# Two gates carried in the rows of a gather table, degrees summed by pairs, and a part of a product moved from VectorE to ScalarE, in a graph network with mixture-of-experts layers

## The reference

```
x = x + gnn0(LN(x))   # product with W, mean over the edges into dst, batch norm, relu
x = x + ffn0(LN(x))   # 256 -> 1024 gelu, top 1 of 8 experts 1024 -> 256
x = x + gnn1(LN(x))   # deg = segment_sum(weight, src) + 1; sum over edges of a src of
                      # LN(x)[dst] * weight * deg^-1/2 * deg^-1/2, then three 256x256 products
x = x + ffn1(LN(x))   # top 2 of 8 experts, softmax of the two logits as gates,
                      # 256 -> 512 relu -> 256
```

## Time and profile before

| | |
|---|---|
| runs | 3897.34, 3900.81, 3908.94 us; median 3900.81 |
| the profiled execution | 3894.43 us, its span 3892.7 us |
| granted TensorE clock, mean | 0.863 |
| busy: PE, DVE, POOL, ACT | 77%, 64%, 59%, 26% of the span |
| first sum | about 116 to 1465 us |
| second sum | about 2235 to 3289 us |
| rest of the last heads and routing | 3289 to 3375 us |
| slots of ffn1 | 3375 us to the end |

### The profile page before, as it was taken

The page is one execution under the profiler, slowest core; times in us unless marked ns, Lnnn a source line. Parts: engine busy times, 40 slices in busy tenths (PEclk is TensorE's granted clock), DMA queues, the critical chain, the costliest instruction groups (busy, mean ns, idle before and its releaser), DMA issues.

```text
span 3892.7 us, 48961 instructions
## 1 busy us (share of the span) xinstructions
PE 2981.4 (77%) x13242; PEld 2223.9 (57%) x13242; DVE 2487.6 (64%) x6393; ACT 1021.9 (26%) x2553; POOL 2284.8 (59%) x2223
## 2 busy tenths in 40 slices
PE   6776766677777777999799077777777776699897
PEld 5665655567676645666688044444544454566554
DVE  5688888898888868664522566666666665633332
ACT  5553433444444415433011200000000000022221
POOL 1676655677777770000244077777777774577776
PEclk9786677899989988999799578888788887799999
DMA  5332222233333332222244433444344445433332
GB/s 160 99 103 85 79 63 64 75 86 86 88 88 87 89 89 76 103 109 98 85 150 135 156 111 116 116 121 116 116 116 121 117 116 85 138 55 55 54 54 44
DMA packets 188761, 380.01 MB, mean 98 GB/s; under 512 B 42140, under 2 KB 113192, under 8 KB 188105
## 3 DMA queue, kind: packets, MB, share of 16 engines
q0 software_dynamic: 121488, 285.06, 28.4%
q1 hardware_dynamic: 58072, 82.67, 6.0%
q10 hardware_dynamic: 8928, 9.04, 0.8%
HBM read 301.05 MB, written 77.44 MB: 97 GB/s over the span
## 4 chain that ended last, share of the span: by engine, by line
PE 44%; DVE 22%; issue 14%; POOL 9%; DMA 8%; DVEq 1%; ACT 1%; SPq 0%; POOLq 0%
PE bank L766 17%; DVE acc_or_weights L733 6%; DMA ring_or_weights<-gather_table,item_other_node 5%; PE bank L1566 5%; PE bank L1383 4%; PE bank L1195 4%; PE bank L934 3%; POOL out_rows L1982 3%; POOL ring_or_weights L777 3%; PE bank L1398 2%; PE bank L1756 2%; POOL normed L1959 2%; PE bank L998 2%; DVE normed L918 2%; DVE acc_or_weights L878 1%
## 5 line engine op out<-in xcount | busy, mean ns | idle before, releaser
L777 POOL DMA_INDIRECT ring_or_weights<-gather_table,item_other_node x1660 | 1664.4, 1003 | 723.6 <-issue 387.2
L733 DVE TENSOR_TENSOR acc_or_weights<-bank,acc_or_weights 128x257 f32 (+1 forms) x1660 | 703.2, 424 | 568.6 <-PE bank L766 479.8
L766 PE MATMUL bank<-ring_or_weights,normed 128*128 128x257 f32 x1660 | 666.0, 490 | 235.2 <-issue 146.2
L766 PE MATMUL bank<-ring_or_weights 128*128 128x256 f32 x1660 | 627.0, 488 | 268.7 <-DVE acc_or_weights L733 96.9
L766 PEld LDWEIGHTS bank<-ring_or_weights 128*128 128x128 f32 x1660 | 319.0, 227 | 537.4 <-issue 286.8
L987 ACT ACTIVATE acc_or_weights<-iota_row,ring_or_weights 128x128 f32<-128x128 f32 x782 | 315.1, 403 | 633.0 <-PE bank L998 623.8
L766 PEld LDWEIGHTS bank<-ring_or_weights,normed 128*128 128x128 f32 x1660 | 307.5, 230 | 287.8 <-issue 273.9
L998 PEld LDWEIGHTS bank<-normed,acc_or_weights 128*128 128x128 f32 x1564 | 352.3, 229 | 78.5 <-ACT acc_or_weights L989 4.6
L934 PE MATMUL bank<-normed 128*128 128x128 f32 x1564 | 254.5, 313 | 139.1 <-DVE normed L922 138.5
L1195 PE MATMUL bank<-identity,normed 128*128 128x128 f32 x1764 | 266.8, 284 | 105.7 <-DVE normed L573 48.6
L1195 PEld LDWEIGHTS bank<-identity,normed 128*128 128x128 f32 x1764 | 213.3, 147 | 187.7 <-issue 82.7
(11 more groups left out here) (337 smaller groups left out, 3955.5 us busy)
## 6 DMA issues: line engine op xcount, KB each, us to landing
ring_or_weights<-gather_table,item_other_node POOLq DMA_INDIRECT x1660, 2.8
hidden_rows<-normed SPq DMA_DIRECT2D x49, 512.0 KB, 2.6
acc_or_weights<-in_L_ffn_Wd SPq DMA_DIRECT2D x8, 1024.0 KB, 5.4
acc_or_weights<-in_L_ffn_W SPq DMA_DIRECT2D x16, 512.0 KB, 9.8
gather_table<-normed SPq DMA_DIRECT2D x7, 896.0 KB, 4.2
gather_table<-acc_or_weights SPq DMA_DIRECT2D x7, 896.0 KB, 4.0
gather_table<-normed SPq DMA_DIRECT2D x24, 256.0 KB, 2.3
out_rows<-x_rows SPq DMA_DIRECT2D x24, 256.0 KB
```

Of the source, the lines that this page charges most:

```text
L733: v.tensor_tensor(into, bank[i % nbank][:, 0:width], into, ALU.add).then_inc(added, 1)
L766: m.matmul(bank[i % nbank][:, 0:width], lhsT=hot, rhs=ring[:, i % RING, 0:width], start=True, stop=True).then_inc(sum_made, 1)
L777: g.indirect_dma_start(ring[:, i % RING, 0:D], None, table, IndirectOffsetOnAxis(ap=gidx[:, i:i + 1], axis=0)).then_inc(ring_in[i % RING], 16)
```

## The change

- **Degrees by pairs.** Two columns of edges are taken together: the one-hots of the tile of both (98 columns) are the weights, and the one-hots of the row of both (256 columns) stream. PE makes 391 products of 98 x 256 instead of 782 of 128 x 49. ScalarE still makes |iota - row| for each column, but relu once for a pair. The sum holds the wanted degrees in two blocks, which two matmuls add at the start of the batch norm stage.
- **A product on ScalarE.** In `spread_edges` the product of lane one-hot and edge values is made by ScalarE (8 activations of 64 columns with a scale read from memory) for all four columns of the first 28 batches and for two of four afterwards. PE sums a batch three items after DVE's step instead of one, and the merge comes two items later.
- **Heads.** Steps fall by 16.5 items for each tile instead of 17, with 12 more items allowed instead of 10. Two steps are added: 11 (Exp on ScalarE) and 12 (three small operations on DVE), which make the head's gates. Items behind the last real one now add to a tile of their own behind tile 48.
- **Gates in the rows.** `tab2` has rows of 258 values: 256 normed and the two gates. A head is stored to it once its gates are there, and after its x. The gate table, its transposes, its store and the 105 gathers of gates are gone. In the slot loop DVE takes the right one of the two gates from the gathered row with two operations on one column.

```diff
-PER_TILE = -(-ITEMS // T)
-MARGIN = 10
+HALVES = 33
+MARGIN = 12
...
-    tab2 = scratch_dram("gather_table2", (T * P, D))
+    tab2 = scratch_dram("gather_table2", (T * P, D + 2))
...
-        v.tensor_scalar(cf, ti, float(T - 1), float(AW), ALU.min, ALU.mult).then_inc(cf_ready, 1)
+        v.tensor_scalar(cf, ti, float((T - 1, T)[k]), float(AW), ALU.min, ALU.mult).then_inc(cf_ready, 1)
...  spread_edges
-        vs.then(v.tensor_tensor(lane_hot[:, 0:n, :], iota[:, 0:LO].unsqueeze(1).broadcast_to([P, n, LO]),
-                                lane_of[:, cols].unsqueeze(2).broadcast_to([P, n, LO]), ALU.is_equal))
-        v.tensor_tensor(spread[:, b % 2, 0:n, :, :], lane_hot[:, 0:n, :].unsqueeze(3).broadcast_to([P, n, LO, 2]),
-                        rec1[:, cols, :].unsqueeze(2).broadcast_to([P, n, LO, 2]), ALU.mult).then_inc(spread_made, 1)
+        if b >= 2:
+            v.wait_ge(spread_scaled, b - 1)
+        lane = lane_hot[b % 2]
+        v.tensor_tensor(lane[:, 0:n, :], iota[:, 0:LO].unsqueeze(1).broadcast_to([P, n, LO]),
+                        lane_of[:, cols].unsqueeze(2).broadcast_to([P, n, LO]), ALU.is_equal).then_inc(spread_made, 1)
+        a = by_scalar(b)
+        if a < n:
+            v.wait_ge(spread_made, lanes_count(b))
+            rest = slice(cols.start + a, cols.stop)
+            v.tensor_tensor(spread[:, b % 2, a:n, :, :], lane[:, a:n, :].unsqueeze(3).broadcast_to([P, n - a, LO, 2]),
+                            rec1[:, rest, :].unsqueeze(2).broadcast_to([P, n - a, LO, 2]), ALU.mult).then_inc(spread_made, 1)
+
+    def by_scalar(b):
+        return min(GC if b < SLOW else GC // 2, batch_columns(b).stop - b * GC)
+
+    def scale_edges(b):
+        s.wait_ge(spread_made, lanes_count(b))
+        if b >= 2:
+            s.wait_ge(spread_summed, b - 1)
+        for c in range(by_scalar(b)):
+            for r in range(2):
+                last = s.activation(spread[:, b % 2, c, :, r], lane_hot[b % 2][:, c, :], ACT.Copy,
+                                    scale=rec1[:, b * GC + c, r:r + 1])
+        last.then_inc(spread_scaled, 1)
...  beside_first_scalar
+            s.activation(lo_tmp[:, i % 2 * P:(i % 2 + 1) * P], iota[:, :], ACT.Abs, bias=neg_lo[:, i:i + 1]).then_inc(lo_abs, 1)
+            if i % 2:
+                s.wait_ge(lo_abs, i + 1)
+                if k >= 2:
+                    s.wait_ge(deg_done, k - 1)
+                s.activation(lo_hot[:, k % 2, :], lo_tmp, ACT.Relu, bias=1.0, scale=-1.0).then_inc(lo_done, 1)
+        for b in batches_due(i):
+            scale_edges(b)
...  beside_first_tensor
-            m.matmul(bank[7][:, 0:T], lhsT=lo_hot[:, j % 2, :], rhs=tile_hot[:, j // HOTS % 2, j % HOTS, :],
-                     start=j == 0, stop=j == EC - 1).then_inc(deg_done, 1)
+            m.matmul(bank[7][0:2 * T, 0:2 * P], lhsT=tile_hot[:, j // HOTS % 2, c:c + 2, :].rearrange("p c t -> p (c t)"),
+                     rhs=lo_hot[:, j // 2 % 2, :], start=j == 1, stop=j == EC - 1).then_inc(deg_done, 1)
-        for b in batches_due(i - 1):
+        for b in batches_due(i - 3):
             sum_spread(b)
...  route_vector
-        vs.then(v.tensor_copy(gate_row[:, 0:slots], got))
-        vs.then(v.tensor_scalar(second, got, float(T * P), -float(T * P), ALU.is_ge, ALU.mult))
-        vs.then(v.tensor_tensor(got, got, second, ALU.add))
+        if l:
+            v.tensor_scalar(is_first, got, float(T * P), None, ALU.is_lt)
+            vs.then(v.tensor_scalar(is_second, got, float(T * P), None, ALU.is_ge))
+            vs.then(v.scalar_tensor_tensor(got, is_second, -float(T * P), got, ALU.mult, ALU.add))
...  heads
-        return PER_TILE * min(T, G2 * (gi + 1)) + MARGIN + 1 + STEP * n
+        return HALVES * min(T, G2 * (gi + 1)) // 2 + MARGIN + 1 + STEP * n
+            for gi in due(when, 12, i):
+                v.tensor_scalar(sum_of, exp, 1.0, None, ALU.add).then_inc(gates_made, 1)
+                v.wait_ge(gates_made, 3 * gi + 1)
+                v.reciprocal(first, sum_of).then_inc(gates_made, 1)
+                v.wait_ge(gates_made, 3 * gi + 2)
+                v.tensor_tensor(more, exp, first, ALU.mult).then_inc(gates_made, 1)
...  second_sync, after the store of x
+            y.wait_ge(gates_made, 3 * gi + 3)
+            y.wait_ge(applied2, gi + 1)
+            y.dma_start(tab2[a * P:(a + n) * P, :].rearrange("(t p) d -> p t d", p=P),
+                        norm2[:, gi % 3, 0:n, :]).then_inc(hid_stored[gi % 3], 16)
...  the slot loop
+                v.tensor_scalar(slot_gate[:, i % 2, 1:2], xg[:, i % NX, D + 1:D + 2], is_second[:, i:i + 1], None,
+                                ALU.mult).then_inc(gate_taken, 1)
+                v.scalar_tensor_tensor(slot_gate[:, i % 2, 0:1], xg[:, i % NX, D:D + 1], is_first[:, i:i + 1],
+                                       slot_gate[:, i % 2, 1:2], ALU.mult, ALU.add).then_inc(gate_taken, 1)
-            if i >= NGATE:
-                g.wait_ge(f_out, i - NGATE + 1)
-            g.indirect_dma_start(slot_gate[:, i % NGATE, :], None, gate_d,
-                                 IndirectOffsetOnAxis(ap=gate_row[:, i:i + 1], axis=0)).then_inc(ring_in[NX + i % NGATE], 16)
```

## The result

The kernel after takes 3856.4 us (median of 6 runs, 3853.6 to 3863.7), the kernel before 3899.7 us beside it (6 runs, 3894.0 to 3908.9). The ratio is 0.9886 with a 95% interval of 0.9872 to 0.9899: 43 us less, where 45 were forecast. The profiled execution has a span of 3851.8 us, 40.9 less than that of before.

A forecast was written before the change was run, and what follows sets the result against it. Bounds: DVE before item 404, POOL otherwise in both sums, landings of additions in the last stage. Savings 18 + 9 + 14.4 + 4 + 1.3 + 0.7, less 0.4, 1.4 and 0.6, give 45 us: 3856 us forecast, range 3838 to 3872.

The forecast's parts named there:

- Product on ScalarE, early batches: First sum, first 28 batches: four product columns leave DVE, the bound there; 18 us saved, bounds 10 and 34.
- Later batches: First sum, 168 batches after item 404: POOL bounds, its gathers shorten with less DVE work; 9 us saved, bounds 0 and 53.
- rival that the whole 45 us come back: Later batches: DVE's overall busyness stretches POOL's gathers, so up to 36 us more are saved, 3820 us; chance 0.10.
- ScalarE's side: Later batches: ScalarE needs 2.9 us a batch against POOL's 3.82, so isn't the bound; cost 0, bound 20 us.
- slower rival: Later batches: ScalarE's hand-over costs over 0.34 us a batch; at 0.5 us, 84 us and 3940 us in all; chance 0.04.
- Degrees by pairs: First sum: PE gets 55 us more work, covered by its waits; no cost, up to 55 us without that cover.
- Heads: Between the second sum's last items and the routing: the last heads end earlier; 14.4 us saved, bounds 8 and 17.
- The gates: Last head's last step to routing: making gates and storing rows takes 3.3 us instead of 2.0; 1.4 us lost, bounds 0 and 3.5.
- Second sum: POOL bounds it, so gate operations and table loads cost 0; new two-input operations stretching gathers cost 0.6 us overall.
- sign that was to show a hindered second sum: Over 1.26 us an item in the second sum would mean table loads or small operations reach POOL, making the prediction wrong.
- Last stage: Additions to the output: the chain of landings bounds at 4.72 us a slot, without gate gathers; 4 us saved, 0 to 6.
- First gathers: Start of the last stage: the first slots start one gate gather earlier, 1.25 us saved.

## Why the prediction was right, step by step

- **Product on ScalarE, early batches.** Forecast 18, measured 20.0, and 19.3 by undoing it. Mechanism and size are right. That it cost nothing to fetch the product from another engine hangs on the three items of lag (14.4 us). The prediction had the lag as a possible gain of up to 17.2 us beside the 18; it is a condition of the 18, and worth about 0.7 us without the move.
- **Later batches.** Forecast 9 of at most 53, by the operations' lengths squared. The pair of traces shows 4.9, undoing it 9.4. The mechanism is shown: equal gaps, shorter gathers, and within one trace gathers stretched by the operations that they start in. The size is some 7 us by those gathers, but the stretches themselves don't repeat well enough to tell 5 from 9. The rival that the whole 45 us come back is excluded by the +30 of the product on DVE.
- **ScalarE's side.** That it doesn't become the bound is right; the price of a product was 0.3 us and is 0.24 in a row, so ScalarE is at 62%. The slower rival needed 0.6 us.
- **Degrees by pairs.** The step that failed: "No cost" was priced at 0, and the edit gives 9 us alone (3 to 14). It rested on PE's time by pieces of a chain at one place, 0.30 us for two columns and 0.44 for a pair, hence 55 us more of PE. The groups have 0.74 and 0.67, 26 us less, beside half the weight loads and a granted clock of 0.90 in place of 0.71 before item 236. So the bound asked only what pairs could cost, and not what they could give.
- **Heads.** 14.4 less 1.4 forecast, 16.8 measured. The term is undersized by 3 to 4 us: the remaining tail ran at a granted clock of 0.73 in place of 0.61, where the prediction took the old steps' times, and at 0.73 on both sides the difference is 13.2 us. The gates cost 1.5 us for a forecast 1.4: from the end of the last selection to the routing are 3.4 us, 1.8 before. Two slips in the prediction's working cancel there: its parts 1.1, 1.7 and 0.3 add up to 3.1 and not 3.3, and the stretch before was 1.84 us and not 2.0.
- **Second sum.** Forecast +0.6 for contention over all, and 0 for gates and table loads; measured +1.8, in a stretch where other kernels with gates by head on chip A have 1056.4 to 1057.8 us, so less than 1.8 may be the change's. The sign that was to show a hindered second sum, over 1.26 us an item, was meant for the gathers' pace, (727.6 + 233.3)/766 = 1.25 us as before; by the milestones both kernels have 1.27. The square root's table is loaded 23 times between 2326 and 3245 us, each time without anybody waiting:

```profile
L561 ACT ACT_TABLE_LOAD  x23: 1283/1283/1283, 2325.8 to 3244.5; - x23
  DVE rstd L555: 114.0, 24
```

  ScalarE: Activation LUTs of the Trainium skill (Table sets) warns of this alternation, with about 5.3 us for two loads. The trace differs: behind the load at 3266.90 us above, the Exp starts at 3268.20, the square root's load at 3268.42 and the square root at 3269.71. That is 2.8 us for two loads of 1.28 and the Exp between them, and no drain shows. In the second sum all of it lies in ScalarE's idle time.
- **Last stage.** Mechanism right and shown three ways; forecast 4, measured 1.3 here and up to 4.3 in other kernels without gate gathers. The term was sized by 4.78 us a slot in a window of 92; over all 104 it was 494.1/104 = 4.75 before, and is 492.8/104 = 4.74, so there were only 0.03 us a slot above the chain's 4.72 to gain. First gathers: 1.0 for 1.25.
- **Not in the sum.** +3.4 us at the very end (below) and +1.5 us in the routing, which repeats in no pattern: 55.0 to 57.3 us over all kernels.

The total was hit to a microsecond because misses balance: 3.9 us before item 236, 2.0 in the early batches and 3.8 at the heads on one side, 4.1 in the later batches, 3.4 at the end, 2.7 in the last stage, 1.5 in the routing and 2.4 in the stretches around the second sum on the other. That leaves the traced execution 4 us above its forecast of 3849 (3853.6). The other 4 went in the step from the traced execution to the median: 6.4 us were added, as in the kernel before, and it was 2.8. The reasoning of the large terms holds; the precision is luck, twice.

The range of 3838 to 3872 is said to have each term at its near bound. Added up, those bounds save 20 to 65 us in place of 45.4, which gives 3836 to 3881; the measured time lies in either.

## What to carry to other kernels

When work is taken off an engine, ask first what waits behind it: here three bounds of 4.75, 4.47 and 4.10 us a slot stood in a row, and 131 us of removed gathers gave 1 to 4 us until the first was loosened, then 33. Work that moves to another engine needs slack where its result is fetched, in the order of the engine that fetches it; three items of lag were 14 of 19 us. Before a contention is priced by a model, sort the victim's instructions by what the other engine is doing when they start: one trace of the kernel before gave 12 of 52 us to the product. And a row of short instructions is priced by the distance of their starts in a timeline, not by the mean duration of a group.

## What the runs showed of the hardware that wasn't expected

- GpSimd's closing drain is longer in the kernel after than before; of the kernel after, and of the kernel before (duration in ns, least, median, most):

```profile
L2040 POOLq DRAIN  x1: 7343/7343/7343, 3844.3 to 3844.3; - x1
```

```profile
L1987 POOLq DRAIN  x1: 3995/3995/3995, 3888.5 to 3888.5; - x1
```

  It takes 4.0 us in the three kernels that gather gates and 7.3 us in the eleven that don't, on every chip, the kernel before without its gate gathers among them. So it is the gathers' absence that costs 3.3 us there; why is open.
- Two additions in flight to one DRAM tensor don't slow each other enough to show: the slot is PE's 4.10 us, where one at a time took 4.75. With the 0.8 us from a landing to the next start, an estimate for the longest landing that fits is 2 x 4.10 - 0.8 = 7.4 us, less than twice the 3.9 of one alone; a smaller slowing wouldn't be seen.
- TensorE was granted 0.90 of its clock on average with the degrees by pairs and 0.71 with single columns, over the same items (0.81 to 0.83 and 0.69 to 0.70 on chips B and C); the fewer, wider products left it busy for 231 us instead of 266.
- Chips differ by 6% on the same kernel (3896 to 4142 us), nearly all of it in stages that gather a row table: 1.27 or 1.48 us an item in the second sum.
- A gather's instruction on GpSimd takes 0.95 us beside an idle DVE or one that adds a bank of PE's, and on average 1.00 to 1.49 us where it starts inside a DVE operation with both operands in SBUF, the longer the more of it is left.
